# Convolution stage of a graph network: scalar loads moved one round ahead on the sync queue, index loads joined in pairs

## The reference, cut to what matters

```python
h = silu(edge_scalars @ W_fc1 / sqrt(10.0))          # 10 scalars of an edge -> 100
w = h @ W_fc2 / sqrt(100.0)                          # 100 -> 128 weights of the edge
w00, w11 = w[:, :32], w[:, 32:64]
w01, w10 = w[:, 64:96], w[:, 96:]
x0e, x1e = y0[edge_src], y1[edge_src]                # the source node's row, gathered
m00 = w00 * x0e * sh0
m11 = w11 * einsum('euc,ec->eu', x1e, sh1) / SQ3
m01 = w01[:, :, None] * x0e[:, :, None] * sh1[:, None, :]
m10 = w10[:, :, None] * x1e * sh0[:, :, None]
sums = segment_sum(concat(m00, m11, m01, m10), edge_dst)
```

## Time and profile before

| what | us |
|---|---|
| median of 3 runs | 9103.93 (9098.42 to 9113.12) |
| span of the profiled execution | 10393.0 |
| first to last gather issue of the convolution | 4640.4 to 7265.8 |
| first to last gather issue of the attention | 7377.8 to 10338.0 |
| POOL busy on the convolution's 1616 gathers | 1574.7 |

### The profile page before, as it was taken

The page is one execution under the profiler, slowest core; times in us unless marked ns, Lnnn a source line. Parts: engine busy times, 40 slices in busy tenths (PEclk is TensorE's granted clock), DMA queues, the critical chain, the costliest instruction groups (busy, mean ns, idle before and its releaser), DMA issues. The chain is left out here.

```text
span 10393.0 us, 195249 instructions
## 1 busy us (share of the span) xinstructions
PE 7790.5 (75%) x51013; PEld 5914.2 (57%) x51014; DVE 6262.0 (60%) x12582; ACT 5115.1 (49%) x9231; POOL 3253.9 (31%) x3274
## 2 busy tenths in 40 slices
PE   5999999787799999976666666667776666666664
PEld 3555555677577777764444444445554444445443
DVE  7989999999433333345555555555555555555556
ACT  3656666787555555543333333333554444444443
POOL 0000000000000000016656555565445555555554
PEclk8999999999899999987777777777887777777776
DMA  3333333666333333321111111111445555555554
GB/s 118 129 126 131 131 128 132 209 225 206 101 122 120 124 119 123 119 71 44 44 44 44 44 44 44 43 45 42 123 141 142 142 146 142 144 142 141 146 140 121
DMA packets 629332, 1179.91 MB, mean 114 GB/s; under 512 B 215323, under 2 KB 289356, under 8 KB 609829
## 3 DMA queue, kind: packets, MB, share of 16 engines
q1 hardware_dynamic: 499978, 861.11, 25.6%
q0 software_dynamic: 129280, 317.93, 11.3%
HBM read 902.02 MB, written 276.57 MB: 113 GB/s over the span
## 5 line engine op out<-in xcount | busy, mean ns | idle before, releaser
L2270 POOL DMA_INDIRECT att_kv_rows<-kv_dram,att_stage x1616 | 1614.3, 999 | 1351.4 <-DVE att_msgs L2413 807.8
L2029 POOL DMA_INDIRECT conv_rows<-y_dram,conv_stage x1616 | 1574.7, 974 | 1060.6 <-DVE conv_msgs L2098 587.7
L694 PE MATMUL conv_part<-conv_msgs,conv_hot 128*128 128x256 f32 x3232 | 1039.1, 474 | 576.3 <-ACT conv_hot L670 375.4
L694 PEld LDWEIGHTS conv_part<-conv_msgs,conv_hot 128*128 128x128 f32 x3232 | 743.4, 242 | 761.0 <-issue 614.9
L2007 ACT ACTIVATE conv_hid<-conv_hid_ps 100x512 f32<-100x512 f32 x408 | 225.4, 594 | 1682.4 <-DMA y_dram<-mean_nodes_both 1304.2
L854 PE MATMUL att_mlp<-late_w,late_hid 128*128 128x128 f32 x3520 | 642.2, 322 | 490.3 <-issue 448.4
L1018 DVE SCALAR_TENSOR_TENSOR mean_rest<-mean_counts,mean_high 128x896 f16<-128x896 f32 x343 | 376.3, 1097 | 1039.2 <-ACT mean_high L979 1039.2
L2241 ACT ACTIVATE acc<-att_q_ps 128x512 f32<-128x512 f32 x404 | 238.3, 590 | 1389.0 <-DMA kv_dram<-conv_nodes_qkv 1165.7
L854 PEld LDWEIGHTS att_mlp<-late_w,late_hid 128*128 128x128 f32 x3520 | 546.4, 226 | 583.4 <-issue 528.7
L694 PE MATMUL att_part<-att_msgs,att_hot 128*128 128x128 f32 x3232 | 595.1, 326 | 302.7 <-issue 254.5
L234 PE MATMUL count_ps<-count_cols,count_rows 128*128 128x392 bf16 x3920 | 743.2, 335 | 74.6 <-DVE count_cols L200 73.6
(11 more groups left out here) (281 smaller groups left out, 16313.4 us busy)
## 6 DMA issues: line engine op xcount, KB each, us to landing
c_dram<-count_counts SPq DMA_DIRECT2D x392, 392.0 KB, 2.3
mean_counts<-c_dram SPq DMA_DIRECT2D x343, 448.0 KB, 3.7
att_w_rows<-w_dram SPq DMA_DIRECT2D x404, 256.0 KB
soft_counts<-c_dram SPq DMA_DIRECT2D x98, 1024.0 KB, 4.8
w_dram<-mlp_w SPq DMA_DIRECT2D x294, 256.0 KB, 2.0
mlp_feats<-in_feats SPq DMA_DIRECT2D x295, 192.0 KB, 2.6
soft_counts<-c_dram SPq DMA_DIRECT2D x49, 1088.0 KB, 5.1
att_lanes<-lo_dram SPq DMA_DIRECT2D x404, 128.0 KB
```

The lines of the kernel that those rows point to most:

```text
L694: ins = nc.tensor.matmul(part, c.hot[:, s, t, :], rows[:, t, :], start=half == 0 and t == 0, stop=half == 1 and t == T - 1)
L2029: pool.indirect_dma_start(rows[:, s, t, :], None, y_dram, bass.IndirectOffsetOnAxis(ap=stage[:, s, t:t + 1], axis=0)).then_inc(gathered[s] ...
L2270: pool.indirect_dma_start(kv_rows[:, s, t, :], None, kv_dram, bass.IndirectOffsetOnAxis(ap=stage[:, s, t:t + 1], axis=0)).then_inc(gathere ...
```

## The change

SP's loop is taken apart into two helpers. `next_scalars(p, i)` waits until PE has read the scalars of pair p of round i and loads those of round i + 1. `next_indices(h, i)` waits for the gathers of both groups of half h of round i and loads the indices of both for round i + 1 in one transfer of 128 x 8. Two calls of `next_scalars` stand ahead of the loop; in it `next_scalars` runs for round i + 1 ahead of `next_indices` for round i. The loop has one round less, so that the indices of a round after the last are no longer loaded. The index buffer has the same bytes in two halves, with one semaphore for each half, and POOL waits for indices ahead of groups 0 and 2 alone.

```diff
--- before.py
+++ after.py
@@ -1916,7 +1916,7 @@
 
         c = LaneSums(nc, st, "conv", iota, spans, acc, 2 * D, banks=2)
         rows = sb("rows", [P, S, T, D])
-        stage = sb("stage", [P, S, T], i32)
+        stage = sb("stage", [P, 2, 2 * T], i32)
         scalars = sb("scalars", [P, 2, GE])
         harm = sb("harm", [P, NT, 4])
         w1 = sb("w1", [P, 100])
@@ -1938,7 +1938,7 @@
         hid_done = sem("conv_hid_done")
         w_done = sem("conv_w_done")
         msg_done = sem("conv_msg_done")
-        staged = [sem(f"conv_staged{s}") for s in range(S)]
+        staged = [sem(f"conv_staged{h}") for h in range(2)]
         gathered = [sem(f"conv_gathered{s}") for s in range(S)]
         scalars_in = [sem(f"conv_scalars_in{p}") for p in range(2)]
 
@@ -1979,26 +1979,34 @@
                     for n in range(2):
                         sp.dma_start(scalars[rows_of(n), p, :], a["scalars"][:, bass.ds((g + n) * GE, GE)]).then_inc(scalars_in[p], 16)
 
-                def load_indices(s, g):
-                    sp.dma_start(stage[:, s], a["src_tiles"][:, bass.ds(g * T, T)]).then_inc(staged[s], 16)
-
-                for s in range(S):
-                    load_indices(s, s)
+                def load_indices(h, g):
+                    sp.dma_start(stage[:, h], a["src_tiles"][:, bass.ds(g * T, 2 * T)]).then_inc(staged[h], 16)
+
+                def next_scalars(p, i):
+
+                    sp.wait_ge(hid_sum, S * i + 2 * p + 2)
+                    load_scalars(p, S * (i + 1) + 2 * p)
+
+                def next_indices(h, i):
+
+                    sp.wait_ge(gathered[2 * h], 16 * T * (i + 1))
+                    sp.wait_ge(gathered[2 * h + 1], 16 * T * (i + 1))
+                    load_indices(h, S * (i + 1) + 2 * h)
+
+                for h in range(2):
+                    load_indices(h, 2 * h)
                 for p in range(2):
                     load_scalars(p, 2 * p)
-                with sp.Fori(0, NI) as i:
-                    for s in range(S):
-
-                        sp.wait_ge(gathered[s], 16 * T * (i + 1))
-                        load_indices(s, S * (i + 1) + s)
-
-                        if s % 2 == 1:
-                            sp.wait_ge(hid_sum, S * i + s + 1)
-                            load_scalars(s // 2, S * (i + 1) + s - 1)
+                for p in range(2):
+                    next_scalars(p, 0)
+                with sp.Fori(0, NI - 1) as i:
+                    for h in range(2):
+                        next_scalars(h, i + 1)
+                        next_indices(h, i)
                 for p in range(2):
                     sp.wait_ge(scalars_in[p], 32 * (NI + 1))
-                for s in range(S):
-                    sp.wait_ge(staged[s], 16 * (NI + 1))
+                for h in range(2):
+                    sp.wait_ge(staged[h], 16 * NI)
 
             @block.scalar
             def _(act):
@@ -2021,14 +2029,15 @@
             def _(pool):
                 with pool.Fori(0, NI) as i:
                     for s in range(S):
-                        pool.wait_ge(staged[s], 16 * (i + 1))
+                        if s % 2 == 0:
+                            pool.wait_ge(staged[s // 2], 16 * (i + 1))
 
                         pool.wait_ge(rows_used, S * i + s + 1)
                         pool.sem_inc(turn, 1)
                         for t in range(T):
                             pool.indirect_dma_start(
                                 rows[:, s, t, :], None, y_dram,
-                                bass.IndirectOffsetOnAxis(ap=stage[:, s, t:t + 1], axis=0)).then_inc(gathered[s], 16)
+                                bass.IndirectOffsetOnAxis(ap=stage[:, s // 2, s % 2 * T + t:s % 2 * T + t + 1], axis=0)).then_inc(gathered[s], 16)
 
             @block.tensor
             def _(pe):
```

## The result

| | before | after |
|---|---|---|
| median of 6 runs, us | 9104.76 (9092.93 to 9113.12) | 9136.61 (9133.85 to 9144.45) |
| ratio of the medians | | 1.0035 (1.0024 to 1.0047) |
| span of the profiled execution, us | 10393.0 | 9136.1 (own time 9137.92) |

The change makes the kernel **slower by 0.35%**, some 32 us. The forecast was 9097 and the range 9035 to 9122: the measured time lies above it, and the change went the other way.

A forecast was written before the change was run, and what follows sets the result against it. POOL's gathers were taken to set the pace of convolution and attention. Scalars each round 0, indices 0, counts 0 and the last round -7 took the median 9104 to 9097 us, with a range of 9035 to 9122.

The forecast's parts named there:

- POOL at its pace of 5.05 us a group: In the convolution, POOL's gathers plus "issue" idle time were taken as 2039 us, 5.05 us for each of 404 groups.
- the term put at 0: In each convolution round, loading scalars a round earlier ends PE's wait but gains 0, since POOL has cover.
- The thin pieces: Convolution and attention stretches with PE and DVE idling in "issue", taken as the profiled execution's own cost, nearly its extra 1289 us.
- POOL sets the pace: In convolution and attention, without the profiled execution's extra idling, POOL's gathers set the pace: 2039 and 2153 us.
- The room of 104 us: At most some 104 us of a timed run are POOL's waits in both stages, what lies around the span included.
- Indices 0: Ahead of groups 0 and 2, POOL's cover for index loads falls from 10.9 to 5.9 us, costing 0.
- counts 0: SP issues 202 index loads fewer and POOL has two waits a round fewer, for a gain of 0.
- 500 times the bytes: Against late index loads: the slowest kind of row takes 5.1 us with 500 times an index load's bytes.
- The last round, 7 us: Behind the convolution's last gather, early scalars shorten the end from 16.7 to 9.6 us, gaining 7 us once.
- PE's wait for scalars goes: In the convolution, PE's waits for scalars at line 2038 (now 2047) would be gone but for the start.
- The faster rival: POOL does wait in the convolution for late scalars; the change takes 20 to 104 us, 9000 to 9077; chance 0.28.
- The slower rival: POOL waits for indices ahead of groups 0 and 2, giving 9137 or, at every load, 9299; chance 0.08.

The follow-up runs named there:

- the first experiment: The kernel before, unchanged, run once more with a profile of its own: 9107.14 us, beside 9109.04 for the median of 22 runs of before.
- the third experiment: The changed kernel with DVE's `tensor_reduce` (L2109) moved up from sixth to third in a message: 9125.74 us, 1.0018 against before.
- the last run: The changed kernel with its two long multiplications (L2106, L2112) reading weights from PSUM, not their scaled copy in SBUF: 9002.84 us, 0.9889 against before.

## Why the prediction was wrong

It failed in one step: "Moving the load a round earlier takes away PE's wait and gives the kernel **0** in each round", which rests on "POOL at its pace of 5.05 us a group". Everything up to the word "gives" held. But the gather's duration was taken as a constant, the same in both kernels, and it depends on what DVE does when the gather starts. Each hold costs about 0.37 us (1664.0 less 1616 x 0.944, over 377), the change makes 108 more of them, and 108 x 0.37 is 40 us; 38.3 were measured. So the term put at 0 was +38 us, and the sum of the prediction's own terms, 0 + 0 + 0 - 7, should have been some +31. The number 5.05 was itself from the disturbed execution; in an undisturbed one the pace is 5.24 before and 5.34 after.

By its other steps:

- **The thin pieces** belong to the profiled execution: right, by the first experiment. The sum was rightly made against the median. But the same argument should have warned that rows 4's 974 ns for a gather came from the disturbed execution too. Where DVE is slowed, its operations meet gathers in other places: that execution has 115 long gathers, the undisturbed one 269.
- **POOL sets the pace**: right. Its idle time is 500.6 to 501.6 us in every one of the undisturbed profiles above, nearly all of it the 0.30 us between two gathers.
- **The room of 104 us**: right as far as waits go (21.0 + 48.4 + 16.3 + 1.8 = 87.5 us in the undisturbed execution). Of these the convolution's 22.8 are no longer than a gap each and could not be won. But the room was in the wrong quantity. What could be won in the convolution with right results (1625.8 less 1530.9, 95 us) was inside POOL's busy time, where no view of waits looks.
- **Indices 0, counts 0**: right (0.9999, and 0.6 us of POOL's waits). "500 times the bytes" was counted from an index load of before, 2 KB; the change's has 4 KB, so it is some 270 times, which alters nothing here.
- **The last round, 7 us**: right, 6.2. The end behind the last gather, 9.6, was put too low (11.8), by the same error in both kernels.
- **PE's wait for scalars goes**: right, 473.5 us to 18.3.
- **The faster rival** (POOL waits for what hangs on scalars): wrong; there was no such wait to win. Its range, 9000 to 9077, is also counted from 9104 at one end and from 9097 at the other.
- **The slower rival** had 8% and the right sign by the wrong way: POOL never waited for indices.

A rule that bears on this was there to be read. The Trainium skill ("SBUF — State Buffer", Who interferes with whom) says that a VectorE instruction with two SBUF inputs contends with a GpSimd instruction that reads SBUF, and that the later of the two waits; `tensor_reduce` is said never to contend on trn2. This case's traces agree in all three points, if an indexed gather, which takes its indices from SBUF, counts as such an instruction. With both inputs in SBUF 376 gathers of after are held, with one of them in PSUM none, and none of the 401 that start under the reduction. The later one waits: a gather that starts before L2106, or in its first 0.02 us, isn't held, and L2106 then takes up to 0.62 us in place of 0.55. The same passage infers that a `tensor_tensor` doesn't stall transfers issued by GpSimd, since writing descriptors needs another interface; for gathers, whose indices lie in SBUF, the measurement decides otherwise.

The trace of before could have told it: rows 1 give 999 ns for a mean gather of the attention and rows 4 give 974 in the convolution, while rows 6, 7 and 8 show single ones of 0.94. A mean above its single rows means that some gathers are longer, and the question what makes them so was not asked.

## What to carry to other kernels

Where one engine's instructions set the pace, look at the spread of their durations as well as at their waits: a mean over the median is a cost that no wait shows. On an engine with slack, what matters can be when an operation runs and which memories it reads; a wait taken away can put two engines in step for the worse, and the fix is then to reorder the operations and keep the edit (here -41 us in place of +32). Before a step is costed at nothing because it is hidden, ask what it makes run beside the pacing engine.

## What the runs showed of the hardware

- An indexed gather of 128 rows takes 0.944 us on POOL (median of after). One that starts while VectorE is already running a `tensor_tensor` of 128 x 384 with both inputs in SBUF ends 0.81 to 0.83 us after that operation's end (376 of 376 in after) and takes at most 1.36 us. Run freely, a gather has 0.82 us left 0.12 us after its start; an operation that ends within that time costs nothing. L2112 of after ends 0.05 us after the start of the gather at 5723.22, which took 0.94; 191 gathers of after start so, with 0.06 us or less of L2112 left, and none is held.
- An operation with one of its two inputs in PSUM (522 gathers start inside one in the last run), or a reduction (401 in the third experiment), doesn't hold it.
- VectorE pays little: L2106 takes 564 ns in the mean in after, and 547 with its weights in PSUM. It pays when the gather starts first, up to 618 ns.
- The attention's gathers show the same sign: mean 1035 ns in after, shortest 940. Of its 1616, 209 are long, and each of these ends 0.81 to 0.83 us after the end of a `tensor_tensor` on VectorE. How much of this can be had by the same means was not tried.
- One profiled execution was 1289 us longer than the runs (10393.0 against 9104), with PE and DVE idle in places for nothing that the profile names ("issue" ahead of DVE's first operation of a message: 201.5 us, against 0.2 in the second profile); the same kernel profiled again had none of it.
